# Expert outputs of a decoder block: scattered with addition onto two tables instead of onto four planes

## What is computed

```
x = x + self_attention(layernorm(x))            # 16 heads, a hyperbolic distance as score
x = x + cross_attention(layernorm(x), ctx)      # 16 heads, context of 512
h = layernorm(x)
logits = -|h - keys|^2 + h @ rw.T + rb          # 16 experts
w, topi = softmax(top_k(logits, 4)), indices
hidden = gelu(h @ w1[e].T + b1[e]);  out_e = hidden @ w2[e].T + b2[e]
x = x + sum over the 4 chosen experts of w * out_e
```

## Time and profile before

| | |
|---|---|
| device time, median of 3 runs | 886.62 us (886.38 to 892.05) |
| the profiled execution | 891.15 us, of which the span of the profile is 889.1 us |
| expert stage, first turn of rows to last matmul | 692.85 to 860.43 us |
| from there to the end of the span | 28.7 us |
| bytes moved by DMA | 56.62 MB, mean 64 GB/s |

### The profile page before, as it was taken

One profiled execution on the slowest core, in us unless ns is written; L12 is line 12 of the kernel. 1 busy time (PEld: TensorE's weight loads), 2 busy tenths in 40 slices (PEclk: granted clock), 3 DMA queues, 4 the chain that ended last, 5 costly groups with the idle time before them and its releaser, 6 DMA issues.

```text
span 889.1 us, 16678 instructions
## 1 busy us (share of the span) xinstructions
PE 710.9 (80%) x5484; PEld 471.4 (53%) x5484; DVE 670.4 (75%) x1642; ACT 579.5 (65%) x770; POOL 489.4 (55%) x578
## 2 busy tenths in 40 slices
PE   3335668787787787999999999999980799999970
PEld 2134346455464464444544444444430799999970
DVE  4669999999999998788789888888444355555534
ACT  2525899899999988145675766766641477777740
POOL 2225786877977885415043464553557266666660
PEclk9855555565565555569999999999995799999995
DMA  9970000000000200050230110000005122222219
GB/s 295 336 244 0 1 1 1 1 0 1 1 1 1 72 1 1 1 191 3 86 99 25 32 32 21 23 14 14 25 25 190 46 82 77 83 74 83 74 54 236
DMA packets 63011, 56.62 MB, mean 64 GB/s; under 512 B 9712, under 2 KB 57200, under 8 KB 62800
## 3 DMA queue, kind: packets, MB, share of 16 engines
q1 hardware_dynamic: 53648, 43.04, 16.7%
q0 software_dynamic: 5056, 10.43, 3.5%
q10 hardware_dynamic: 4224, 2.10, 1.0%
HBM read 25.97 MB, written 29.57 MB: 62 GB/s over the span
## 4 chain that ended last, share of the span: by engine, by line
PE 58%; DVE 22%; issue 9%; POOL 4%; DMA 3%; ACT 2%; ACTq 1%; DVEq 0%; SPq 0%; POOLq 0%
PE ops L1204 7%; PE slot L1309 7%; PE slot L1180 5%; PE slot L1017 5%; DVE S_YZ L1458 4%; PE bps L1322 4%; DVE S_FB L1429 4%; PE ops L1322 4%; PE slot L1188 4%; DVE S_YZ L1447 3%; PE bps L1054 3%; PE tps L1166 3%; DVE X_junk L1488 3%; PE ops L1040 2%; POOL rows L689 2%
## 5 line engine op out<-in xcount | busy, mean ns | idle before, releaser
L571 POOL TENSOR_TENSOR S_YZ<-S_YZ 128x512 f32<-128x512 f32 x128 | 189.4, 1516 | 60.1 <-ACT S_YZ L775 59.9
L826 ACT ACTIVATE B_W<-slot 128x1024 f32<-128x1024 f32 x128 | 131.2, 1026 | 92.0 <-PE slot L1188 92.0
L1488 DVE CUSTOM_DVE_ANT_0 X_junk<-tps,X_MB 128x512 bf16<-128x512 f32 x240 | 156.2, 688 | 32.2 <-PE tps L1166 31.3
L723 POOL DMA_INDIRECT picks<-F_ROUT,F_GOAL x94 | 104.8, 1115 | 72.5 <-DVE F_ROUT L1823 54.4
L1017 PE MATMUL slot<-S_UQT,S_UKT 32*128 32x256 f32 x256 | 81.4, 471 | 64.1 <-DVE S_YZ L1447 62.8
L1458 DVE SCALAR_TENSOR_TENSOR S_YZ<-S_YZ 128x1024 f32<-128x1024 f32 x64 | 109.0, 1722 | 0.0
L1017 PEld LDWEIGHTS slot<-S_UQT,S_UKT 32*128 32x128 f32 x256 | 54.9, 295 | 92.8 <-DVE S_YZ L1447 74.5
L689 POOL DMA_INDIRECT rows<-B_ROW,B_IDX x64 | 63.0, 985 | 48.6 <-DVE B_ROW L1559 28.3
L1429 DVE TENSOR_SCALAR S_FB<-slot 128x512 f32<-128x512 f32 x112 | 74.8, 684 | 17.2 <-PE slot L1021 16.4
L1021 PE MATMUL slot<-S_GQT,S_GKT 32*128 32x256 f32 x256 | 82.5, 440 | 0.0
L1166 PE MATMUL tps<-X_KFT,X_QFT 24*128 24x512 f32 x240 | 79.4, 520 | 3.4 <-DVE X_MX L1488 1.1
(11 more groups left out here) (289 smaller groups left out, 1596.7 us busy)
## 6 DMA issues: line engine op xcount, KB each, us to landing
rows<-S_blank SPq DMA_DIRECT2D x17, 1040.0 KB, 12.4
F_RIN<-rows SPq DMA_DIRECT2D x47, 130.0 KB, 2.1
B_W<-w1T SPq DMA_DIRECT2D x16, 256.0 KB, 4.4
F_W<-w2T SPq DMA_DIRECT2D x16, 256.0 KB, 5.0
X_CT<-ctxT SPq DMA_DIRECT2D x8, 256.0 KB, 4.6
B_W<-picks SPq DMA_DIRECT2D x8, 256.0 KB, 8.6
B_W<-picks ACTq DMA_DIRECT2D x8, 256.0 KB, 8.8
picks<-F_ROUT,F_GOAL POOLq DMA_INDIRECT x94
```

The costliest lines, as they stand in the source:

```text
L571: g.tensor_tensor(Y[:, n % YR], Y[:, n % YR], Zr[:, n % ZR], ALU.add).then_inc(f_rdy, 1)
L723: g.indirect_dma_start(out=picks[:, :], out_offset=bass.IndirectOffsetOnAxis(ap=GOAL[:, s, i:i + 1], axis=0), in_=ROUT[:, s, i, :], in_off ...
L826: act.activation(W[:, at:at + 2, 2 * j:2 * j + 2, :].rearrange("p h t n -> p h (t n)"), E_BANKS[k % 2][:, :, :], ACT.Exp, scale=SCALE).the ...
L1488: dve.tensor_tensor_reduce(out=junk[:, i, :], in0=bank, in1=MB[:, c % 2, t, :], scale=1.0, scalar=-3.0e38, op0=ALU.add, op1=ALU.max, accum ...
```

## The change

The destination is no longer one DRAM tensor of four planes but two, `sums[0]` and `sums[1]`, each with 2048 rows for the tokens and 256 spare ones. Row NT*p + t of a table is the token in slot t of partition p, so that a partition's 16 rows lie one behind the other (8 KB). All four choices of a token carry the same id. Tile t is scattered with addition (`compute_op=ALU.add`) onto table t % 2; before its issue GpSimd waits until tile t-2, the one before on the same table, has landed. Table 1 begins with zeros, written in the fill at the start, with the spare rows of both; table 0 begins with X, stored after the last batch of the cross attention. At the end there are 8 loads of 256 KB, table 0 by SyncE and table 1 by ScalarE's queue, in pieces of 2 KB, and one addition of DVE for each quarter, which writes X. The tile `room` only keeps the addresses of the tiles behind PAD as they were.

```
-        picks = nc.dram_tensor("picks", (TOPK * CAP + TILES * SLOTS, D), F32, kind="Internal").ap()
+        sums = [nc.dram_tensor(f"sums{i}", (CAP + SLOTS, D), F32, kind="Internal").ap() for i in range(2)]
+        FILLS = E + 1 + 3
...
-        PAD, PAD_F = sB("PAD", [TILES, 2], I32), sB("PAD_F", [TILES, 2])
+        PAD, PAD_F = sB("PAD", [2], I32), sB("PAD_F", [2])
+        sB("room", [4 * TILES - 4])
...
+        def plane(j):
+            return sums[j][0:CAP, :].rearrange("(p t) d -> p t d", t=NT)
...   # SyncE, behind the 17 fills
+            sp.dma_start(plane(1), blank[:, 0:1, 0:D].broadcast_to([P, NT, D])).then_inc(fill_done, 16)
+            for i in range(2):
+                sp.dma_start(sums[i][CAP:CAP + SLOTS, :].rearrange("(p i) d -> p i d", i=2), blank[:, :, 0:D]
+                             ).then_inc(fill_done, 16)
...   # the waits for fill_done now want 16 * FILLS
             sp.wait_ge(*t_emptied("proj", B - 1))
+            sp.dma_start(plane(0), X[:, :, :]).then_inc(sum_in, 16)
             for e in range(W2_EARLY, E):
                 load_w2(e)
...   # the loads at the end
-                for j in (0, 2):
-                    sp.dma_start(ZT[:, q, j], picks[j * CAP + q * 512:j * CAP + q * 512 + 512, :]
-                                 .rearrange("(t p) d -> p t d", p=P)).then_inc(z_in[q], 16)
+                sp.dma_start(ZT[:, 0, 4 * q:4 * q + 4], plane(0)[:, 4 * q:4 * q + 4, :]).then_inc(z_in[q][0], 16)
...
-                for j in (1, 3):
-                    act.dma_start(ZT[:, q, j], picks[j * CAP + q * 512:j * CAP + q * 512 + 512, :]
-                                  .rearrange("(t p) d -> p t d", p=P)).then_inc(z_in[q], 16)
+                act.dma_start(ZT[:, 1, 4 * q:4 * q + 4], plane(1)[:, 4 * q:4 * q + 4, :]).then_inc(z_in[q][1], 16)
...   # GpSimd
-            ch.step(g.iota(PAD[:], pattern=[[SLOTS, TILES], [1, 2]], base=TOPK * CAP, channel_multiplier=2))
+            ch.step(g.iota(PAD[:], pattern=[[1, 2]], base=CAP, channel_multiplier=2))
...
-                g.iota(AT_I[:], pattern=[[P, TN], [CAP, TOPK]], base=c * N, channel_multiplier=1).then_inc(at_rdy, 1)
+                g.iota(AT_I[:], pattern=[[1, TN], [0, TOPK]], base=c * TN, channel_multiplier=NT).then_inc(at_rdy, 1)
...
+            g.wait_ge(sum_in, 16)
             for t in range(TILES):
                 s = t % NR
                 g.wait_ge(goal_rdy, t + 1)
                 g.wait_ge(y_rdy2, t + 1)
+                if t >= 2:
+                    g.wait_ge(rout[(t - 2) % NR], 32 * ((t - 2) // NR + 1))
                 for i in range(2):
-                    g.indirect_dma_start(out=picks[:, :], out_offset=bass.IndirectOffsetOnAxis(
-                        ap=GOAL[:, s, i:i + 1], axis=0), in_=ROUT[:, s, i, :], in_offset=None).then_inc(rout[s], 16)
+                    g.indirect_dma_start(out=sums[t % 2][:, :], out_offset=bass.IndirectOffsetOnAxis(
+                        ap=GOAL[:, s, i:i + 1], axis=0), in_=ROUT[:, s, i, :], in_offset=None,
+                        compute_op=ALU.add).then_inc(rout[s], 16)
...   # DVE
-                dve.tensor_tensor(GOAL[:, s, :], RIN[:, s, :, D], PAD_F[:, t, :], ALU.min).then_inc(goal_rdy, 1)
+                dve.tensor_tensor(GOAL[:, s, :], RIN[:, s, :, D], PAD_F[:, :], ALU.min).then_inc(goal_rdy, 1)
...
-                dve.wait_ge(z_in[q], 16 * TOPK)
-                xq = X[:, 4 * q:4 * q + 4, :]
-                for j in range(TOPK):
-                    i = dve.tensor_tensor(xq, ZT[:, q, j], xq, ALU.add)
-                    if j < TOPK - 1:
-                        rch.link(i)
-                i.then_inc(z_sum, 1)
+                for j in range(2):
+                    dve.wait_ge(z_in[q][j], 16)
+                v = slice(4 * q, 4 * q + 4)
+                dve.tensor_tensor(X[:, v, :], ZT[:, 0, v], ZT[:, 1, v], ALU.add).then_inc(z_sum, 1)
```

More of the change, by code:

```diff
@@ L326, in decoder_block @@
         HB = sF("HB", [2, FC, SLOTS])
-        ZT = W[:, :, :, :].rearrange("p a b c -> p (a b c)").rearrange("p (q j t d) -> p q j t d", q=NT // 4, j=TOPK, t=4)
+        ZT = W[:, 0:4, :, :].rearrange("p a b c -> p (a b c)").rearrange("p (j t d) -> p j t d", j=2, t=NT)
         topF.close()
@@ L345, in decoder_block @@
         h_full, h_rdy, y_full, y_used, y_rdy2 = sem("h_full"), sem("h_rdy"), sem("y_full"), sem("y_used"), sem("y_rdy2")
-        z_in = [sem(f"z_in{i}") for i in range(TB)]
+        z_in = [[sem(f"z_in{q}_{j}") for j in range(2)] for q in range(TB)]
+        sum_in = sem("sum_in")
         z_sum, out_done = sem("z_sum"), sem("out_done")
@@ L460, in _ @@
             sp.wait_ge(s_done, B)
-            sp.wait_ge(fill_done, 16 * (E + 1))
+            sp.wait_ge(fill_done, 16 * FILLS)
             for dst, src in ((keysT[:, :], a["keysT"]), (rwT[:, :], a["rwT"]), (rb_b[:, :], a["rb"].partition_broadcast(P)),
@@ L653, in _ @@
             g.wait_ge(s_done, B)
-            g.wait_ge(fill_done, 16 * (E + 1))
+            g.wait_ge(fill_done, 16 * FILLS)
             ch.step(g.memset(ones[:, :], 1.0))
```

## The result

The changed kernel takes **896.75 us** (median of 6 runs, 893.29 to 900.7) and the kernel before, beside it on the same chip, 887.46 (6 runs, 886.38 to 892.05). The ratio is **1.0107, 95% interval 1.0085 to 1.0128**: slower by 1.1%, or 9.3 us between the medians, where -7.0 us was forecast. Its profiled execution took 894.93 us, with a span of 892.9.

A forecast was written before the change was run, and what follows sets the result against it. PE was taken to bound the expert stage at 3.43 us a tile, DMA the final reads. From 886.62 us, -10.1 (end), +1.6 (last scatters) and +1.5 (RIN waits) gave -7.0: 879.6 us, range 875.5 to 882.5, whole range to 905.

The forecast's parts named there:

- the price of an issue with addition: GpSimd's scatters: addition adds 0.25 us to each issue of 0.97, so a tile's pair just fits in 3.43.
- R1: Expert stage: scatter issue grows by half to 1.45 us, GpSimd's period 3.50 exceeds PE's 3.43; 883.7 us; chance 0.12.
- The gap of 0.70: GpSimd, ahead of each pair of scatter issues: 0.70 us from last input to issue, counted within the 3.43 tile.
- The page cited: Skill page on DMA addition: two reads and one write, three descriptors for two; an issue growing with them gives 883.7 us.
- Landing: Scatters with addition: landing takes 0.6 us more; with dearer issues the pair takes 4.8 us instead of 3.7.
- The end of the stream: Behind the last matmul: four issues at 0.25 us more each, plus 0.6 for landing, cost +1.6 us.
- RIN ring: Six RIN buffers in the expert stage: loads start 1.1 us later, tiles with little lead wait; +1.5 us in all.
- R2: Expert stage: scatter pair grows by 1.8 to 2.45 us, so every load of RIN is late; 885.0 us; chance 0.13.
- The new wait: GpSimd's wait for tile t-2 to land: costs nothing, since 5.5 us fit in two tiles' 6.86, cover 1.35.
- R3: Expert stage: from 2.45 us pair growth, GpSimd's wait for tile t-2 ends last; about 917 us; chance 0.27.
- The end (-10.1): After the last scatter: half the reads, longer pieces, one last addition instead of four, stores included; -10.1 us.
- R4: After the last scatter: start and landing of loads and stores hold the end, only -5 us; 884.7 us; chance 0.07.

The follow-up runs named there:

- Four planes with addition: Kernel before with addition in every scatter onto its four zero-filled planes, no wait between scatters: 925.93 us, ratio 1.0108.
- the loaded GpSimd: Kernel before with idle memsets on GpSimd behind each scatter issue: 920.56 us, ratio 1.0026 with two; 939.15 us, 1.0250 with three.
- half the rows: Changed kernel with both scatter issues of a tile on partitions 0 to 63 only: 899.81 us, ratio 0.9820 to the kernel before.
- half of the additions: Changed kernel with addition only in a tile's first scatter issue, plain write in the second: 899.34 us, ratio 0.9803 to the kernel before.
- the one table: Changed kernel with one table for all tiles, each scatter waiting for the tile just before: 1015.04 us, ratio 1.1065 to the kernel before.
- Two tables with plain issues: Changed kernel with a plain write instead of addition in the scatter, wait kept: 908.22 us, ratio 0.9895 to the kernel before.
- a better layout for plain rows: Kernel before with a token's four plain rows side by side, 4 KB load pieces, 16 additions of four slots on DVE: 910.82 us, ratio 0.9929.

## Why the prediction was wrong

**The step that failed is the price of an issue with addition**: "+0.25 for each issue" was taken, **+0.59** measured (0.97 to 1.56, issues that follow each other). By +0.25, GpSimd's pair "fits in 3.43 with 0.70 ahead of it, just"; by +0.59 it is 3.73 and does not fit. That one number turns -7.0 into a loss. Four planes with addition show that the addition alone gives this pace, and the loaded GpSimd that such a pace alone lengthens the stage.

**Which rival it was.** R1, in its mechanism: GpSimd's period becomes the bound. Its size was too small, half of 0.97 instead of 0.6, and so a period of 3.50, +3.2 in 45 tiles, and 883.7 us. With the measured price the same sum is 45 x 0.30 = 13.5 in the stream (12.8 came) and, as measured, 4.8 behind the last matmul, less 10.1: 886.6 + 8.2 = 894.8, within the runs of the changed kernel. The prediction's own upper bound for an issue was twice 0.97, and 1.56 lies well inside; R1 should have been worked out over that range. It would then have shown that the threshold is at an issue of 1.41 ((3.43 - 2 x 0.30) / 2), 0.44 above the plain one, and that each 0.1 beyond it costs 9 us. Half of the bounds' width lay behind it, and R1 got a chance of 0.12.

**The gap of 0.70 that vanished.** The prediction had "0.70 ahead of it" beside two issues and 0.30, read from a few tiles and taken as needed. The profile after shows 0.30 between all issues as soon as inputs are waiting. So GpSimd could take up to 1.41 for an issue before the stream suffered, more than the 1.22 that the prediction called "just": half the rows, at 1.40, sat at that edge. The trace of before hinted at it: in most tiles the first issue of a pair took 1.41 or more, 0.44 over the second, and PE did not wait.

**The page cited.** By the rule that the prediction took from the Trainium skill, "Collectives: The Full Stack", three descriptors for two gave 1.45 us for an issue; measured are 1.56, so the warning was nearer than the +0.25 chosen over it. As a proportion it is not borne out: half the rows would be half the descriptors, and still take 1.40.

**Landing.** From the start of a pair's second issue to its landing it is 3.21 in the tile shown and 3.26 at the end, where the earlier trace rows has 2.24 and the prediction's ordinary tile 2.44 (795.71 to 798.15). That is +0.8 to +1.0; of it +0.6 is the issue's own growth and 0.2 to 0.4 the landing's, less than the 0.6 taken. The whole pair took 1.87 + 3.21 = 5.1 where 4.8 were forecast: the excess is the issues'.

**The end of the stream** was put at +1.6 (four issues at 0.25, 0.6 for landing). Measured +4.8. Five issues start behind the last matmul, where four start at it or behind it in the kernel before, since GpSimd was one behind: four steps of 1.865 (869.70 to 877.16) and 3.26 to landing, against three of 1.27 and 2.24. That is 1.8 for the longer steps, 1.9 for one step more, 1.0 for the last issue with its landing, 0.1 for the start.

**RIN ring (+1.5, R2).** PE does wait for RIN in most tiles, which was named as R2's sign. But the ring only hands on GpSimd's pace: the loaded GpSimd has a long stage with plain landings, and half of the additions little of it. R2's delay is a part of R1 here, not a cause beside it.

**The new wait (nothing; R3, "about 917").** Right that it costs nothing: 1.5 us in all on GpSimd. R3's slope is real, as the one table shows with a turn of 5.97; two tables allow 7.46. The cover of 1.35 came out as 1.5. "Slower" got 0.24, but by this mechanism, which is not the one that made it slower.

**The end (-10.1)**: exactly that, 22.6 to 12.5. Reads went at 360 GB/s where 340 was taken between the rates of the earlier trace rows; the one addition took 0.69; R4 is out. Two tables with plain issues have it too (12.2).

**At nothing**: the store of X, the fills, ids and PAD. The issue of that store took 0.34 us on SyncE, and the stage began no later than before, at 689.19 against 692.85; nothing is seen of the others.

## What to carry to other kernels

Where an engine's work per tile is near the pace of the bound, work out the threshold first (here an issue of 1.41 us against 3.43 a tile) and ask how much of an unknown price's range lies behind it: below it the price is free, behind it each tile pays. An engine that only issues DMAs can become the bound through a ring of buffers, and then the waits are named after the ring and not after it; loading that engine with idle work, or halving the suspect, tells the two apart, best on a chip on which a trace of the kernel before is at hand. A reduction handed to the DMA can cost the engine that issues it more than the saved reads give back; a better layout for plain rows gave some 3 us of the end alone.

## What the hardware showed that was not expected

- An indirect scatter of 128 rows of 512 bytes with addition takes GpSimd 1.56 us to issue in the median (up to 2.03), plain 0.97 (up to 1.48); with addition and 64 rows 1.40. Landing behind the last issue: 3.26 us against 2.24. By the totals of the queue, added rows go as packets of a row, plain ones by eights.
- GpSimd's least gap between two such issues is 0.30 us, whether inputs are new or not.
- On three chips the kernel before took 915 to 917 us instead of 887. Kernels with plain scatters have stalls of 2.6 us on ACT and DVE in the expert stage there, and the granted clock from 500 to 660 us is 0.95 to 0.98 over all kernels, where the first chip has 1.00. The same change is +1.07% on the first and 0.9985 (0.9959 to 1.0012) on another. The cause stays open.
- Two additions of DVE and GpSimd at the same time took DVE's from 425 to 826 ns each, in the median.
